# Two graph layers and two mixtures: attention's scores turned to rows, ACT rescales, and GpSimd holds two transfers in flight

## What is computed

```python
# layer 0: relational attention (8 relations, 4 heads of 64), normalised input x
feat_all = einsum('ni,rhid->rnhd', x, conv_weights)
e = leaky_relu(el[type, src] + er[type, dst], 0.2)      # 4 scores per edge
m = segment_max(e, dst); ex = exp(e - m[dst])
h = segment_sum(ex / segment_sum(ex)[dst] * feat_all[type, src], dst) + h_bias
# layer 1: shared MLP + 4 experts, top 2
# layer 2: messages: filter(edge_attr) * x[dst], summed over src, two dense layers, batch norm
# layer 3: 16 experts (256 -> 512 -> 256, gated), top 2 of 16
```

## Time and profile before

| | us |
|---|---|
| median of 3 runs | 4172.16 (4170.39 to 4174.0) |
| profiled execution, its time | 4176.44 |
| its span | 4174.7 |
| POOL busy | 2277.2 (55%) |
| PE / DVE / ACT busy | 2928.3 / 2177.3 / 1210.5 |

### The profile page before, as it was taken

One profiled execution on the slowest core, in us unless ns is written; L12 is line 12 of the kernel. 1 busy time (PEld: TensorE's weight loads), 2 busy tenths in 40 slices (PEclk: granted clock), 3 DMA queues, 4 the chain that ended last, 5 costly groups with the idle time before them and its releaser, 6 DMA issues. The chain is left out here.

```text
span 4174.7 us, 73619 instructions
## 1 busy us (share of the span) xinstructions
PE 2928.3 (70%) x20296; PEld 2364.7 (57%) x20297; DVE 2177.3 (52%) x5961; ACT 1210.5 (29%) x3266; POOL 2277.2 (55%) x2336
## 2 busy tenths in 40 slices
PE   5199101777777777776379679999999864299990
PEld 1188101555555555555255358888888633288990
DVE  8411002877777777777743557777777444011112
ACT  1123000444444444444223223333333231022220
POOL 2777775777777777777240056666666200511115
PEclk8599655998998999999679789999999875599995
DMA  3344101222222222225100143333335501155533
GB/s 105 108 135 137 40 2 32 63 65 63 63 64 63 64 64 63 64 64 62 23 19 1 47 136 89 90 89 90 90 90 84 52 0 39 49 175 173 171 104 114
DMA packets 209214, 317.71 MB, mean 76 GB/s; under 512 B 63367, under 2 KB 150063, under 8 KB 208388
## 3 DMA queue, kind: packets, MB, share of 16 engines
q0 software_dynamic: 95008, 179.89, 19.9%
q1 hardware_dynamic: 103204, 127.24, 9.4%
q10 hardware_dynamic: 10944, 9.97, 0.7%
HBM read 248.03 MB, written 68.84 MB: 76 GB/s over the span
## 5 line engine op out<-in xcount | busy, mean ns | idle before, releaser
L1402 POOL DMA_INDIRECT conv_got<-xtab,conv_rowidx x588 | 565.8, 962 | 313.2 <-DVE conv_msg L1507 156.6
L806 POOL DMA_INDIRECT att_got<-feat,att_rowidx x588 | 573.2, 975 | 201.5 <-issue 150.2
L294 POOL DMA_INDIRECT table<-l0a_rec,l0a_addr x469 | 458.2, 977 | 216.7 <-issue 146.1
L1454 PE MATMUL conv_pf<-conv_wf,conv_act 128*128 128x256 f32 x2352 | 534.0, 380 | 0.2 <-DVE conv_filt L1502 0.2
L812 POOL DMA_INDIRECT table<-recs_rec,recs_addr x432 | 423.2, 980 | 131.6 <-issue 130.4
L1454 PEld LDWEIGHTS conv_pf<-conv_wf,conv_act 128*128 128x128 f32 x2352 | 447.6, 190 | 76.9 <-issue 0.8
L982 PE MATMUL att_pmax<-all_identb,att_away 128*128 128x512 bf16 x588 | 261.1, 444 | 203.9 <-DVE att_elo L901 203.2
L863 DVE TENSOR_REDUCE att_tmax<-att_pmax 128x4 f32<-128x512 f32 x588 | 373.8, 680 | 31.1 <-PE att_pmax L986 27.6
L986 PE MATMUL att_pmax<-all_identb,att_ehi 128*128 128x128 bf16 x2352 | 383.6, 242 | 0.0
L986 PE MATMUL att_pmax<-all_identb,att_elo 128*128 128x128 bf16 x2352 | 383.3, 242 | 0.0
L1420 ACT ACTIVATE conv_act<-conv_p,conv_bf 128x512 f32<-128x512 f32 x294 | 186.2, 684 | 552.1 <-PE conv_p L1446 552.1
(11 more groups left out here) (336 smaller groups left out, 5074.0 us busy)
## 6 DMA issues: line engine op xcount, KB each, us to landing
moe_w<-in_L_ffn_w SPq DMA_DIRECT2D x96, 512.0 KB
feat<-proj_out SPq DMA_DIRECT2D x30, 1040.0 KB
results<-moe_y ACTq DMA_DIRECT2D x76, 128.0 KB, 1.7
att_got<-feat,att_rowidx POOLq DMA_INDIRECT x588
conv_got<-xtab,conv_rowidx POOLq DMA_INDIRECT x588, 2.8
xtab<-ln_row SPq DMA_DIRECT2D x60, 128.0 KB, 1.7
table<-l0a_rec,l0a_addr POOLq DMA_INDIRECT x469
table<-recs_rec,recs_addr POOLq DMA_INDIRECT x469, 2.1
```

What stands on the lines that cost most here:

```text
L294: self.nc.gpsimd.indirect_dma_start(out=self.table, out_offset=bass.IndirectOffsetOnAxis(ap=self.addrs[:, j:j + 1], axis=0), in_=self.recs ...
L806: nc.gpsimd.indirect_dma_start(out=got[g % 3][:, k, :], out_offset=None, in_=feat, in_offset=bass.IndirectOffsetOnAxis(ap=rowidx[:, g * K ...
L1402: nc.gpsimd.indirect_dma_start(out=got[g % 3][:, k, :], out_offset=None, in_=xtab, in_offset=bass.IndirectOffsetOnAxis(ap=rowidx[:, g * K ...
L1454: ins = nc.tensor.matmul(pf[b][:, k, :], act1[s3][:, h, (2 * b + k) * P:(2 * b + k + 1) * P], wf2[:, h, :], start=(h == 0), stop=(h == 1))
```

## The change

It limits the indirect transfers and rebuilds the score path of `att`:

- `Transfers`, with LIMIT 2: before GpSimd issues a transfer it waits until the transfer before the last has landed. It holds in `Sender` (all scatters to both tables), in `att`, in `conv` and in `send`; not in `moe` and `comb`. Each of the four gathers of a group gets a semaphore of its own.
- Table 1's columns are split anew: 214 in `att` (none in the first four groups, then 1 and 2 in turn), 12 in `join`, 26 in `ln1`, 24 in `route0`, 167 in `mixf`, 26 in `ln2` (before: 432 in `att`, 37 in `mixf`).
- Scores are written spread into a [128, 4, 32] bf16 tile (high and low parts), turned by four PE transposes into rows (`pE`), copied by ACT (`eT`), and each column's `pmax` takes one 512-column matmul with `select` in place of eight of 128.
- One DVE reduction over all four columns replaces four; the running maximum is read in place.
- ACT multiplies the accumulator by `keep` (four activations into `shrunk`); DVE then does one addition of 260 columns in place of four multiply-adds.
- The pipeline is 4 deep in place of 3, with four buffers for what is gathered; the sums come one step later. The relation masks `typ` are made once for all columns before the loop, and `acc` is cleared after the row numbers are cast.

```diff
+class Transfers:
+    LIMIT = 2
+    def room(self):
+        if len(self.order) >= self.LIMIT:
+            self.pool.wait_ge(*self.order[-self.LIMIT])
+    def begun(self, name, sem):
+        self.counts[name] = self.counts.get(name, 0) + 16
+        self.order.append((sem, self.counts[name]))
...
-COLS1 = ROUND * (ET // K - 3), EJ - ROUND * (ET // K - 3)
+COLS1 = ET // K - 4 + (ET // K - 4) // 2, 12, 26, 24, 167, 26
...
# attend, GpSimd
+            sends = [0 if g < SLOTS else 1 + g % 2 for g in range(GROUPS)]
             for g in range(GROUPS):
-                if g >= SLOTS:
-                    pool.wait_ge(f_ready, g - 2)
-                    pool.wait_ge(last_ready, (g - 2) * LAST)
                 for k in range(K):
+                    if g >= SLOTS and k == 0:
+                        pool.wait_ge(f_ready, g - SLOTS + 1)
+                    if g >= SLOTS and k == ON_DVE:
+                        pool.wait_ge(last_ready, (g - SLOTS + 1) * LAST)
+                    under_way.room()
                     nc.gpsimd.indirect_dma_start(out=got[u][:, k, :], ...
...
# attend, DVE
-            for k in range(K):
-                dve.wait_ge(max_ready, g * K + k + 1)
-                count(v.tensor_reduce(tmax[:, k, :], pmax[k][:, :, :], AX.X, ALU.max))
+            dve.wait_ge(max_ready, g + 1)
+            v.tensor_reduce(tmax[:, :], pmax[:, :, :, :].rearrange("p k h e -> p h k e"), AX.XY, ALU.max)
...
# attend, PE
-                        for h in range(HEADS):
-                            for part in (ehi, elo):
-                                nc.tensor.matmul(pmax[k][:, h, :], part[s1][:, k, h:h + 1].broadcast_to([P, P]), c["identb"][:, :], ...
+                        nc.tensor.matmul(pmax[:, k, :, :], select[:, k:k + 1].broadcast_to([ROWS, P]), eT[(u - 1) % 2][:, :, :], ...
...
# convolve, GpSimd
-                if g >= SLOTS:
-                    pool.wait_ge(msg_ready, (g - 2) * 2)
                 for k in range(K):
+                    if g >= SLOTS and k % 2 == 0:
+                        pool.wait_ge(msg_ready, (g - SLOTS) * 2 + k // 2 + 1)
+                    under_way.room()
```

More of the change, by code:

```diff
@@ L735, in attend @@
     LAST = (K - ON_DVE) * HEADS
-    N_DV = (1, 5, K + 4, HEADS - 1)
-    three = range(SLOTS)
+    ROWS = 2 * K * HEADS
+    four = range(SLOTS)
     with Stage(nc, "att") as s:
@@ L769, in attend @@
-        er_ready, e_ready, max_ready, drop_ready = (s.sem(n) for n in ("er_ready", "e_ready", "max_ready", "drop_ready"))
+        shrunk = s.sb("shrunk", [P, HEADS, H1])
+        select = s.sb("select", [ROWS, K], BF16)
+        pmax = s.ps("pmax", [P, K, HEADS, P])
+        pT, pE = s.ps("pT", [P, 1024], BF16), s.ps("pE", [ROWS, 1024], BF16)
+        terms = s.ps("terms", [P, 2, K, 2 * RELS * HEADS])
+        per, pme = terms[:, 0, :, :], terms[:, 1, :, :]
+        psum = s.ps("psum", [P, 512])
@@ L786, in in_steps, with bin_of @@
                 peeled(t)
[L787 to L790, removed]
+            with eng.Fori(2, GROUPS // SLOTS) as i:
+                for u in four:
+                    step(i * SLOTS + u, i, u, set(range(DEPTH + 1)))
+            for t in range(GROUPS // SLOTS * SLOTS, GROUPS + DEPTH):
                 peeled(t)
+        def bin_of(eng, g):
+            return eng.value_load(bins0[0:1, bass.ds(g, 1)], min_val=0, max_val=NT - 1)
@@ new lines, in step @@
+                if 1 in parts:
+                    g = t - 1
+                    act.wait_ge(spread_turned, g + 1)
+                    wait_positive(act, max_ready, g - 1)
+                    nc.scalar.activation(flat(eT[(u - 1) % 2][:, :, :]), pE[:, 0:HEADS * P], ACT.Copy).then_inc(eT_ready, 1)
+                if 3 in parts:
+                    for k in range(ON_DVE + 1, K):
+                        products(k)
+                if 4 in parts:
+                    g = t - 4
+                    bin4 = bin_of(act, g)
+                    wait_positive(act, acc_done, g)
+                    act.wait_ge(keep_ready, g + 1)
+                    for h in range(HEADS):
+                        nc.scalar.activation(shrunk[:, h, :], flat(acc[:, bass.ds(bin4, 1), h, :]), ACT.Copy,
+                                             scale=keep[s4][:, h:h + 1]).then_inc(shrunk_ready, 1)
```

408 lines of the change are left out of this document (206 added, 202 removed).

## The result

| | before | after |
|---|---|---|
| median, us | 4171.27 (4 runs, 4166.4 to 4174.0) | 5026.24 (4 runs, 5018.27 to 5033.74) |
| span of the profiled execution | 4174.7 | 5026.0 |
| mean granted clock | 0.858 | 0.748 |

The ratio is 1.2051, 95% interval [1.2029, 1.2073]: slower by a fifth. The forecast was 4251, its range ended at 4375. The direction was right, the size was not.

The account below looks back on a forecast made before the run. It took transfers to pace `att`, PE to bound `conv`, and GpSimd's scatters to end `proj`. Terms 10 + 62 - 78 + 0 + 11 + 3 + 18 + 53 = +79 on 4176.4, less 4.3 for the median, gave 4251 us; range 4125 to 4375.

Parts of the forecast that it names:

- Item 4: `att`, compute: rebuilt score path takes 7.2 to 7.8 us a group, hidden under the transfers, so saves nothing of its own.
- 8.19: Forecast us of transfers for an average `att` group, 4 gathers at 1.57 and 1.5 scatters at 1.27; 8.94 before.
- Rival 3: Score path becomes `att`'s bound at the lower clock, step 9.0 to 9.3, `att` +40 us, total 4370; chance 0.10.
- Item 8: `conv`: a full group takes 6.1 us in place of 5.84, +35; with padding and the end +53 (+10 to +95).
- L: Time from a transfer's start to its landing; taken as 2.8 us in `conv`, 2.1 for a scatter.
- r: Time from a landing to the start of the transfer waiting for it, taken as 0.27 us; a pair takes L + r.
- Item 3: `att`, transfers: fewer scatters make groups shorter, -80 us; with start -3 and drain +5, -78.
- Item 2: `proj`: scatters go 1.74 us apart beside `feat`'s stores, leaving 49 for afterwards, +62 us (0 to +90).
- Rival 2: Scatters beside stores are slow: `proj` +90 to +110 us, `ln0` +25, scatters of `att` +20, total 4330; chance 0.11.
- Items 1, 5, 6, 7, 9: Scatters in `ln0` +10 us, `join` +11, `ln1`, `route0` and `ln2` +3 together, `mixf` +18, `send` 0.
- Rival 1: Round trips are shorter with fewer under way: `att` -165 us, all -115, total 4060; chance 0.19 with rival 4.
- Rival 4: The rebuild counts, not the transfers: `att` gains over 1 us a group, -150 or more; counted with rival 1.

Follow-up runs that it names:

- e15: The changed kernel with DVE's addition moved ahead of the maximum and ACT's rescaling moved, nothing else (32 rows, two under way): 4661.71 us, ratio 1.1164.
- e9: The changed kernel with four transfers under way in place of two: 4728.63 us, ratio 1.1341.
- e14: e11 with `eT` and `select` on 32 rows again: 4311.98 us, ratio 1.0346.
- e7: The changed kernel with `eT` and `select` on 128 rows in place of 32, the added ones zero: 4963.13 us, ratio 1.1902.
- e11: The changed kernel with the addition ahead of the maximum, `eT` and `select` on 128 rows, and four transfers under way: 4177.15 us, ratio 1.0016.
- e8: The changed kernel with the addition ahead of the maximum and `eT` and `select` on 128 rows, two under way: 4609.77 us, ratio 1.1053.
- e10: The kernel before with the limit of two under way and the changed kernel's waits, old score path and split: 4760.47 us, ratio 1.1416.
- e6: The changed kernel unaltered, run again beside the kernel before: 5031.31 us, ratio 1.2063.
- e13: The changed kernel with `conv` waiting for both message halves ahead of a group's first gather, not its third: 4958.11 us, ratio 1.1883.
- e16: e11 with table 1 split anew, one message wait a group in `conv`, and `att`'s tile-number loads moved earlier: 4128.94 us, ratio 0.9900.
- e1: The changed kernel with four under way, on the chip where the kernel before took 5281.74 us: 5282.99 us.
- e2: The changed kernel with addition and rescaling moved earlier in `att` and `conv`'s message wait one gather earlier, on the 5281.74 us chip: 4872.87 us.
- e4: The kernel before with the limit of two and the changed kernel's waits, on the chip where it took 5281.74 us without: 4851.66 us.

## Why the prediction was right or wrong

- **Item 4 is the step that failed.** It compared each engine's busy time with 8.19 and named one chain on PE ("m -> `pme` -> sums -> `pmax`, about 3 us"), "the whole step at 7.2 to 7.8, hidden". It mentioned that `shrunk` releases DVE's addition and didn't follow what the addition releases: the next sums, in the one bank, and behind them `pme`, which DVE waits for. The loop so runs over two engines: all of DVE's work stands in it, and PE's sums behind it instead of beside it. Measured 12.30; -78 became +506 with the start and the drain. Moving the addition and the rescaling gave 370 us back (e15), 417 with four under way (e9 to e14). The price it gave (15 us for each 0.1 us over 8.19) makes +616 of the 4.11 us over, so +538 with its -78, where +506 came. Its own sign of being wrong, waits of `att` for PE or ACT, is what the trace shows. No run gives the sums a second bank: what is shown is the order.
- **The sizes within item 4 were right**: the reduction takes 2.29, as forecast; the addition takes 0.42 where the four multiply-adds took 0.86 (0.3 less forecast); DVE is busy for 501 in 1000 us, 6.2 a group of 12.3 (5.7 forecast). Busy time was not the question.
- **The clock.** Rival 3 had it (lower level, chain doubled) at 0.10, and priced it at +40. Its argument against, "PE at 0.72 had 0.91", is what failed: at 0.73 of busy time the changed kernel has 0.62, and with 0.93 it has 0.62 too (e14). The four score matmuls fill 32 rows; on 128 rows the clock is 0.79 (e7) and 0.90 (e11). Alone that is 68 us, with the order mended 135. With the order mended and the low clock left, the step is 9.62 (e14) and 9.80 (e15), close to the rival's 9.0 to 9.3. The Trainium skill (TensorE: Matmul & The Clock Gate, Part 4: PE-mode transpose) says that transposes don't count as a busy PE in the same way. No run here takes them away; they stayed in e7 and e11, and the clock rose, so they alone don't hold it down here.
- **Item 8** had the mechanism and L (2.7 to 2.9), and mis-sized r, read off a start that waited for DVE, 0.27. Landings give 0.22 to 0.3 where the transfer has no other wait, and 0.73 to 0.8 where it has two. With 0.75 a pair is 3.55 and the group 7.1, 133 x 1.26 = +168 in place of +35. Measured +212 in all, 7.21 a group. Most of the rest is padding: in the last 14 groups a gather lands in 3.5 to 4.3 us (4061 to 4143), not 0.5 over 2.8, and a group takes 8.82, not 7.3, another 21 us.
- **Item 3**: the transfers of `att` never showed in the changed kernel. Where they do, its 8.19 was too low: e8, with order and rows mended, takes 9.34 (8.60 with four under way, e11). In e10 a transfer is 1.54, scatters included, and not 1.27: a scatter that follows gathers waits for a gather's landing (0.83 of idle time at 1535.48).
- **Item 2**: mechanism right, L mis-sized (3.6 for 3.2), so a pace of 1.92 beside stores for 1.74: +88.5 for +62. Some 8 of the 26 us fell ahead of the stores, at 172 to 212, where the forecast had none (21 scatters for 27). **Rival 2** had +90 to +110 for this stage and came close there, but its scatters of `att` didn't show.
- **Items 1, 5, 6, 7, 9** held within 7 us each (`send` takes 74.7 from first to last scatter, 74.8 before). In `join` the Trainium skill (SBUF — State Buffer, Practical consequences), by which a `tensor_tensor` of two SBUF inputs was not seen to stall a transfer's descriptors, would have given 0; the scatters took 8.30, 7.89 and 7.88, against 0.96 free. The trace disagrees, as the earlier trace rows did.
- **Rival 1** falls: nothing landed earlier for fewer under way, 2.6 as the least in `conv` before and after; the 2.3 that the figures of the Trainium skill (DMA: Bandwidth & Descriptors, Anatomy of one DMA — SWDGE path) give for 128 KB, an estimate, is not reached. **Rival 4** falls the other way: the rebuild lost. The range (to 4375) left this out because every case in it kept the step near 9. That the change came out slower, as 0.76 had it, is in part luck: of +79 forecast `att` was -78, and its +506 came by a path that no item had.

## What to carry to other kernels

An engine's busy time bounds a step from below only. Before calling a rebuilt stage hidden, walk every buffer that exists once (here a PSUM bank) round the engines: what frees it, what that instruction stands behind in its own queue, and what stands behind the one that waits. And don't price the clock by the busy share of the old matmuls: here fewer and longer ones on 32 rows had another clock at the same share.

## What the runs showed of the hardware

- Four bf16 matmuls of 512 columns a group on 32 rows in place of 128 (the other 96 zeros), nothing else changed: granted clock 0.61 against 0.79 (e6, e7), 0.62 against 0.90 (e14, e11).
- A transfer on GpSimd with two waits ahead starts 0.73 to 0.8 us after the landing, with one 0.22 to 0.3 (e13, and after).
- Two loads of a register from SBUF on DVE stand with 0.32 and 0.72 us of its idle time where they are apart (e11) and 0.82 together (e16); the 0.69 us of one-hot ahead of them in e16 didn't hide them.
- Scatters with two under way land in 3.6 us as a median beside `feat`'s stores and in 2.1 after them (after).
- One chip took 5282 us for a kernel that three others ran in 4169 to 4173. There, while scatters ran 1.26 apart in `proj` (e1), ACT's steps came 11.2 us apart. With a limit of two scatters are 1.96 to 1.99 apart there, and ACT's steps are as on the other chips (e2 to e4). In `mixf` scatters stay 1.28 apart under the limit, and it stayed slow (e2: 383 us from its first scatter to that of `ln2`, some 220 after). Its cause stays open.
